# Thirty-two dense ranges instead of twenty-eight in a graph network's layer 1, with VectorE clearing the stored ranges and weighting late one-hots

## The reference

```python
x = ln(x + segment_sum(w_e * x[dst], src) @ W0.T)           # layer 0: sums by src
# layer 1: two graph convolutions, 128 and 64 features wide
deg  = in-degree + 1;  norm = deg[src]**-.5 * deg[dst]**-.5
h1 = relu(batch_norm(segment_sum(norm * (x @ W1)[src], dst) + b1))
h2 = relu(batch_norm(segment_sum(norm * (h1 @ W2)[src], dst) + b2))
x = ln(x + relu(concat(x, h1, h2) @ Wfc + bfc))
x = ln(x + mlp((1 + eps) * x + segment_sum(w_e * x[src], dst)))      # layer 2
x = ln(x + relu(ln(segment_sum(norm * (x @ W3)[src], dst) + b)))     # layer 3
```

## Time and profile before

| | us |
|---|---|
| median of 3 runs (3447.18 to 3460.74) | 3450.46 |
| the profiled execution | 3453.26 |
| its span, first to last instruction | 3452.0 |
| spread stage, first scatter to last | 45 to 1250 |
| layer 1's first pass (its POOL and PE work) | 1410 to 1749 |
| layer 1's second pass | 1794 to 2121 |
| layer 2's pass and tail | 2230 to 2935 |
| layer 3's pass and tail | 2935 to 3452 |
| busy: PE, POOL, DVE, ACT | 2833.8, 2463.3, 2001.4, 1170.1 |

### The profile page before, as it was taken

The page is one execution under the profiler, slowest core; times in us unless marked ns, Lnnn a source line. Parts: engine busy times, 40 slices in busy tenths (PEclk is TensorE's granted clock), DMA queues, the critical chain, the costliest instruction groups (busy, mean ns, idle before and its releaser), DMA issues. The chain is left out here.

```text
span 3452.0 us, 60131 instructions
## 1 busy us (share of the span) xinstructions
PE 2833.8 (82%) x19220; PEld 2088.0 (60%) x19220; DVE 2001.4 (58%) x7356; ACT 1170.1 (34%) x2749; POOL 2463.3 (71%) x2237
## 2 busy tenths in 40 slices
PE   5999877788888869789977997777888876699995
PEld 4777655566666648444446774356666665466664
DVE  7999888886777639442243434443444564235557
ACT  4354554566877748200010002500111232001113
POOL 3888778876776667677747776777777774777774
PEclk9999999999999979899978997589999998799997
DMA  8787888888888889678856886755556564988884
GB/s 273 112 142 107 150 158 153 158 154 174 181 174 174 178 185 347 180 211 234 236 132 177 227 223 171 217 174 156 163 177 182 161 177 122 299 237 247 251 250 141
DMA packets 658434, 652.77 MB, mean 189 GB/s; under 512 B 87902, under 2 KB 606476, under 8 KB 656588
## 3 DMA queue, kind: packets, MB, share of 16 engines
q0 software_dynamic: 153600, 258.41, 37.6%
q1 hardware_dynamic: 430670, 331.83, 31.2%
q10 hardware_dynamic: 73854, 58.70, 5.4%
HBM read 434.19 MB, written 214.52 MB: 188 GB/s over the span
## 5 line engine op out<-in xcount | busy, mean ns | idle before, releaser
L1680 POOL DMA_INDIRECT A<-rows_buf,big x572 | 900.6, 1574 | 327.8 <-issue 149.0
L880 POOL DMA_INDIRECT rows_buf<-T,idx x888 | 852.0, 959 | 275.9 <-issue 273.8
L974 PE MATMUL PSA<-S,rows_buf 128*128 128x128 bf16 (+2 forms) x5904 | 576.6, 252 | 217.9 <-DMA rows_buf<-X,idx 103.3
L974 PEld LDWEIGHTS PSA<-S,rows_buf 128*128 128x128 bf16 (+2 forms) x5904 | 515.9, 140 | 301.6 <-DMA rows_buf<-X,idx 82.4
L880 POOL DMA_INDIRECT rows_buf<-X,idx x528 | 508.2, 963 | 160.9 <-issue 159.4
L1030 DVE TENSOR_TENSOR accT<-PSA,accT 128x256 f32 (+2 forms) x354 | 132.6, 375 | 830.2 <-PE PSA L974 822.9
L1538 DVE TENSOR_TENSOR accT<-PSA,accT 128x392 f32 (+5 forms) x366 | 239.6, 655 | 168.1 <-PE PSA L1473 76.0
L1376 PE MATMUL PSA<-XRS,rows_buf 128*128 128x256 f32 x1144 | 311.2, 396 | 6.2 <-ACT rows_buf L1388 6.2
L791 ACT ACTIVATE accT<-accT,vec 128x500 f32<-128x500 f32 (+3 forms) x26 | 17.7, 694 | 668.4 <-DVE accT L789 668.3
L1388 ACT ACTIVATE rows_buf<-PSA 128x512 f32<-128x512 f32 x286 | 168.7, 594 | 203.9 <-PE PSA L1376 198.5
L1376 PEld LDWEIGHTS PSA<-XRS,rows_buf 128*128 128x128 f32 x1144 | 208.4, 196 | 31.3 <-ACT rows_buf L1367 6.6
(11 more groups left out here) (311 smaller groups left out, 5645.5 us busy)
## 6 DMA issues: line engine op xcount, KB each, us to landing
XRS<-Ad SPq DMA_DIRECT2D x400, 256.0 KB
Ad<-accT SPq DMA_DIRECT2D x224, 196.0 KB
XRS<-in_xpad SPq DMA_DIRECT2D x192, 128.0 KB
Awd<-accT SPq DMA_DIRECT2D x48, 392.0 KB
A<-accT SPq DMA_DIRECT2D x9, 1600.0 KB
rows_buf<-T,idx POOLq DMA_INDIRECT x888
rows_buf<-A SPq DMA_DIRECT2D x24, 512.0 KB
accT<-A SPq DMA_DIRECT2D x24, 512.0 KB, 6.4
```

Source lines behind the costliest of these rows:

```text
L880: s_hg[slot(i)][j // 2].on(pool.indirect_dma_start(Gv(slot(i), j), None, table, bass.IndirectOffsetOnAxis(idx[:, c:c + 1], 0)), 16)
L974: last = pe.matmul(PS[bank_of(i)][0:F, W * h:W * h + W], Gv(slot(i), j)[:, o:o + F], hits[:, i % SRING, j, :], start=j + part == 0, stop=j ...
L1680: s_k[n].on(pool.indirect_dma_start(A, bass.IndirectOffsetOnAxis(tgt[:, c:c + 1], 0), G[:, i % RING, j, :], None, compute_op=ALU.add), 16)
```

## The change

NWIN goes from 28 to 32. HOT becomes 556 chunks, the four new ranges are 32 units of one chunk with slots of 18, and layer 1's passes have 56 groups instead of 64 and eight quadruples of ranges instead of seven. The planner places the units anew: the hot ranges and the eleven beside them end at step 85 instead of 90, DENSE0 is 87 instead of 92, the last unit stays at step 137.

ACT no longer clears the ranges from HWIN on, nor `Aww`. DVE clears `Aww` in one int32 instruction per hot range and the 23 other range buffers that are used again in one bfloat16 instruction each, at the end of step s+4. The hot ranges' counts are still cleared on ACT with their flags; for the others the flag comes from the degrees: four small instructions in `add_flags` test whether a node from block 4 on has a degree over 250. In steps from DENSE0 on, DVE multiplies the one-hots by the weights, in one instruction of 128x512, and ACT does not.

```diff
@@ -40,7 +40,7 @@
 SPAN = 116
 MAXN = 20
 UC = NT * MAXN
-NWIN = 28
+NWIN = 32
 HWIN = 6
 OHRING = 6
 LEAD = 6
@@ -64,7 +64,7 @@
 HOT = BND[NWIN]
 FAR = 16384
 CLASSES = ((0, 64, 4, 8), (64, 120, 2, 8), (120, 160, 2, 10), (160, HOTW, 1, 8),
-           (HOTW, 376, 2, MAXN), (376, 448, 1, 14), (448, HOT, 1, 16))
+           (HOTW, 376, 2, MAXN), (376, 448, 1, 14), (448, 524, 1, 16), (524, HOT, 1, 18))
 G0 = BND[XWIN] // CG
 NCOLD = NG - 1 - G0
 ORDER = [x for i in range(HWIN) for x in (i, HWIN + i)][:2 * HWIN - 1]
@@ -179,6 +179,11 @@
 DENSE0 = cleared_at(HWIN - 1, 3) + 1
 
 
+CLEARED = [w for w in ORDER if w >= HWIN and any(user_before(q) == w for q in range(NWIN))]
+FARBLOCK = window_range(HWIN)[0] // 128
+MOSTDEGREE = 250
+
+
 def dense_step(t):
     return DENSE0 + t * (NCOLD - 2 - DENSE0) // NT
 
@@ -1312,6 +1317,11 @@
             if i >= 2:
                 v.wait_ge(s_M, i - 1)
             v.tensor_tensor(Su[:, i % 2, :, :], iota4, cur16[:, g:g + 1, :].broadcast_to([128, W, CG]), ALU.is_equal).then_inc(s_su, 1)
+            if i >= DENSE0:
+                v.wait_ge(s_su, i + 1)
+                c = CG * g
+                v.tensor_tensor(S[:, i % 2, :, :], Su[:, i % 2, :, :].rearrange("p w j -> p j w"),
+                                wgt[:, c:c + CG].unsqueeze(2).broadcast_to([128, CG, W]), ALU.mult).then_inc(s_sv, 1)
             v.wait_ge(s_sr, i + 1)
             for j in range(CG):
                 last = v.tensor_scalar(Eq[:, i % 2, j, :], PS[0][:, 128 * j:128 * j + 128], srcf[:, g, j:j + 1], 0.0,
@@ -1328,6 +1338,8 @@
 
         def weigh(i):
 
+            if i >= DENSE0:
+                return
             sc.wait_ge(s_su, i + 1)
             if i >= 2:
                 sc.wait_ge(s_M, i - 1)
@@ -1352,7 +1364,10 @@
             for j in range(CG):
                 last = pe.matmul(PS[1][:, 0:W], onesb[:, :], Su[:, i % 2, :, j], start=j == 0, stop=j == CG - 1)
             last.then_inc(s_hp, 1)
-            pe.wait_ge(s_sw, i + 1)
+            if i < DENSE0:
+                pe.wait_ge(s_sw, i + 1)
+            else:
+                pe.wait_ge(s_sv, i - DENSE0 + 1)
             pe.wait_ge(s_eq, i + 1)
             if i >= 1:
                 pe.wait_ge(s_mc, i)
@@ -1523,7 +1538,11 @@
             else:
                 v.wait_ge(s_ae, u.turns[half])
             if u.at - FIRST[u.w].at < 2 and user_before(u.w) is not None:
-                v.wait_ge(s_az, TURN[user_before(u.w)] + 1)
+                before = user_before(u.w)
+                if before < HWIN:
+                    v.wait_ge(s_az, before + 1)
+                else:
+                    v.wait_ge(s_azc, CLEARED.index(before) + 1)
             if u.at - FIRST[u.w].at < 2 and TURN[u.w] == LASTHOT + 2:
                 v.wait_ge(s_azw, HWIN)
             if half:
@@ -1549,17 +1568,23 @@
 
         def window_clear(w, i):
 
-            if w < HWIN and i in (0, 2):
-                sc.wait_ge(s_aww, 16 * (PARTS * w + (2 + i) * PARTS // 4))
-                for b in (i, i + 1):
-                    done = sc.activation(Aww[:, 1568 * b:1568 * b + 1568], nought[:, 0:1].broadcast_to([128, 1568]), ACT.Identity)
-                if i == 2:
-                    done.then_inc(s_azw, 1)
             sc.wait_ge(s_aw[TURN[w] % 2], 16 * (PARTS * (TURN[w] // 2) + (i + 1) * PARTS // 4))
             part = Aw[buffer_of(w)][:, 1568 * i:1568 * i + 1568]
             done = sc.activation(part, part, ACT.Relu, bias=neg255[:, 0:1], accum_out=full[:, 4 * w + i:4 * w + i + 1])
             if i == 3:
                 done.then_inc(s_az, 1)
+
+        def clear_weights(w):
+
+            v.wait_ge(s_aww, 16 * PARTS * (w + 1))
+            part = Aww.bitcast(I32)
+            v.tensor_scalar(part, part, 0, None, ALU.bitwise_and).then_inc(s_azw, 1)
+
+        def clear_counts(w):
+
+            v.wait_ge(s_aw[TURN[w] % 2], 16 * PARTS * (TURN[w] // 2 + 1))
+            part = Aw[buffer_of(w)]
+            v.tensor_scalar(part, part, 0.0, None, ALU.mult).then_inc(s_azc, 1)
 
         def dense_turn(t):
 
@@ -1650,17 +1675,13 @@
                     dense_turned(t)
                     if t + 2 < NT:
                         dense_load(sc, t + 2)
-            for w in ORDER:
+            for w in range(HWIN):
                 for k in range(4):
                     if i == cleared_at(w, k):
                         window_clear(w, k)
             if i == 10:
                 load_weights()
             transfers(i + 2)
-        for w in ORDER:
-            for k in range(4):
-                if cleared_at(w, k) > NCOLD:
-                    window_clear(w, k)
         for p in range(NCOLD + 3, NCOLD + 8):
             transfers(p)
 
@@ -1743,6 +1764,12 @@
                 for u in following[k:k + 1]:
                     onehots(u)
                 additions(us[k + 1:k + 2])
+            for w in range(HWIN):
+                if i == cleared_at(w, 2):
+                    clear_weights(w)
+            for w in CLEARED:
+                if i == cleared_at(w, 2):
+                    clear_counts(w)
             if i == 0:
                 unit_places_known()
             if i == 1:
@@ -1795,7 +1822,7 @@
         for i in range(2):
             sp.wait_ge(s_aw[i], 16 * PARTS * (NWIN // 2))
         v.wait_ge(s_da, NCOLD)
-        v.wait_ge(s_az, NWIN)
+        v.wait_ge(s_az, HWIN)
         v.wait_ge(s_azw, HWIN)
         settle_without_pool()
         for k in range(COPIES):
@@ -1994,6 +2022,11 @@
 
     def add_flags():
 
+        many = full[:, 4 * HWIN:4 * HWIN + 2]
+        link(v.memset(many, 1.0))
+        link(v.tensor_reduce(many[:, 0:1], dnm[:, FARBLOCK:NT - 1], AX.X, ALU.min))
+        link(v.tensor_copy(many[0:rows(NT - 1), 1:2], dnm[0:rows(NT - 1), NT - 1:NT]))
+        link(v.tensor_scalar(many, many, 1.0 / math.sqrt(MOSTDEGREE), None, ALU.is_lt))
         link(v.tensor_reduce(okf[:, 0:1], full[:, :], AX.X, ALU.add))
 
     def overflowed():
```

More of the change, by code:

```diff
@@ L273, in build @@
     early = big[:, 0:2 * LAST]
-    key = early[:, 5568:5568 + HOT]
-    srcm = early[:, 6112:6112 + HOT // 2].bitcast(BF16)
+    key = early[:, 5504:5504 + HOT]
+    srcm = early[:, 6096:6096 + HOT // 2].bitcast(BF16)
     iotak = early[:, 6384:6384 + UC // 2].bitcast(F16)
@@ L301, in build @@
     iota16 = sb("iota16", [128, W], BF16)
-    full = sb("full", [128, 4 * NWIN])
+    full = sb("full", [128, 4 * HWIN + 2])
     okf = sb("okf", [128, 2])
@@ L315, in build @@
     Su = early[:, 4800:5312].bitcast(BF16).rearrange("p (r w j) -> p r w j", r=2, j=CG)
-    lower = early[:, 5376:5504]
-    identb = early[:, 5504:5568].bitcast(BF16)
+    lower = early[:, 5312:5440]
+    identb = early[:, 5440:5504].bitcast(BF16)
     srcl = part[4].bitcast(BF16)[:, 784:1568]
@@ L1909, in build @@
     s_spread = count("s_spread")
-    s_ah, s_am, s_ae, s_az = (nc.alloc_semaphore(n) for n in ("s_ah", "s_am", "s_ae", "s_az"))
+    s_ah, s_am, s_ae, s_az, s_azc = (nc.alloc_semaphore(n) for n in ("s_ah", "s_am", "s_ae", "s_az", "s_azc"))
     s_su, s_sw, s_oq, s_amw, s_aew, s_azw, s_aww = (nc.alloc_semaphore(n) for n in ("s_su", "s_sw", "s_oq", "s_amw", "s_aew", "s_azw", "s_aww"))
     s_aw = [nc.alloc_semaphore(f"s_aw{i}") for i in range(2)]
+    s_sv = nc.alloc_semaphore("s_sv")
     ABW = [XS[:, 2 + i, :].bitcast(BF16) for i in range(2)]
```

## The result

The changed kernel takes 3503.99 us, median of 4 runs (3499.66 to 3509.54), where the kernel before takes 3452.57 on the same chip: a ratio of 1.0153 with a 95% interval of 1.0137 to 1.0169. It is 51 us slower, where 33 us faster was forecast, and lies outside the range. The profiled execution has a span of 3508.3 us. Every figure of a stage here comes from one profiled execution of each kernel.

| stage of the profiled execution, us | before | after | forecast | measured |
|---|---|---|---|---|
| start to degree addition of step 87 | 735.3 | 774.6 | +10 | +39.3 |
| step 87 to step 137 | 454.2 | 471.1 | -15 | +16.9 |
| step 137 to the last one, 142 | 33.5 | 28.7 | -5 | -4.8 |
| from there to the first gather of pass 1 | 187.3 | 193.7 | 0 | +6.4 |
| first pass, to the first gather of the second | 383.7 | 388.3 | +2 | +4.6 |

A forecast was written before the change was run, and what follows sets the result against it. POOL was taken to pace the early spread and layer 1's passes, waits over ACT's copies the late spread. 3453.3 us with 2 - 25 + 10 - 15 - 5 = -33 us gave 3420 us, range 3380 to 3465 us.

The forecast's parts named there:

- The late part: Spread stage, steps 87 to 137: 8.6 us per step, 439 us instead of 454, -15 us, bounds -46 and +25.
- term (d): Spread stage, DVE: 32 more units at 1.4 us each, 45 us; 0.4 us per late step.
- The early part: Spread stage, first 87 steps: 39 us added to DVE, which idles 94 of 705 us; +10 us, bounds 0 and +39.
- The tail: The six spread steps behind step 137, with no clears in ACT's way: -5 us, bounds 0 and -10.
- The first pass: Layer 1: eight groups fewer, but PE takes over at 5.86 us per step; 341 us against 339, +2 us.
- The second pass: Layer 1: DMA transfers at a 0.96 share set 5.3 us per step; 302 us against 327, -25 us.
- Rival 1: Spread stage: DVE's clears take POOL's time too, late steps stay at 9.4 us; +41 us, 3494 us, 12%.
- Rival 2: Layer 1 passes: DMA share no higher than 0.85, passes +16 and +8, spread -10; 3467 us, 13%.
- Rival 3: Spread stage: only ACT held late steps, now 8.1 us each, early clears fit idle time; -69 us, 3384 us, 14%.
- 4: Whole kernel: gains and costs cancel, spread +5 to +20, second pass -15 to -20; 3440 to 3458 us, 10%.
- 5: Layer 1 passes: new ranges' chunks spill over their slots, left-over loop runs 196 more rounds each; over 900 us more, 1%.
- my signs of being wrong: Late steps under 8.1 or over 9.2 us, scatters beside a clear over 3 us, or the second pass not shrinking.

The follow-up runs named there:

- the narrow units: Changed kernel with 32 ranges, first 12 turns spaced as with 28, instructions of the last four ranges' units 98 columns wide: 3501.95 us, 1.0127.
- 28 ranges respaced: Kernel before, nothing added, first 12 turns spaced as with 32 ranges, so the 12th ends with step 85: 3483.18 us, 1.0079.
- fewer bytes: Changed kernel loading half of each piece of counts in both layer 1 passes (but for the first pieces), all products done: 3470.90 us, 1.0068.
- less for TensorE: Changed kernel without the middle of three parts of each range's product in pass one and two of three products beside in pass two: 3444.21 us, 0.9987.
- the kernel with reductions: Changed kernel with DVE's clears, all but the sixth of Aww, replaced by one-port maximum reductions of nearly the same length: 3506.65 us, 1.0141.

## Why the prediction was wrong

- **The late part, the step that failed and cost most.** It was to fall to 8.6 us a step: 8.1 us of DVE's work and 0.5 us that I left DVE to idle. It took 9.4 (471.1 / 50). The work was right: DVE is busy 407.4 us of these, 8.15 a step. What failed is the idle time: 63.7 us, 1.27 a step. I had put the new units, term (d), into time in which DVE idles. The late parts of the kernel with the moves and 28 ranges and, in the second fence, with 32 ranges in the same spacing (columns as in the earlier trace rows) show that this didn't happen:

```profile
754.60:1216.60 462.00, 383.85 (x2555) 316.79 (x2554) 377.58 (x1224) 204.02 (x419) 354.60 (x212) 0.94 0.89 180
```

```profile
755.30:1267.70 512.40, 407.50 (x2619) 323.75 (x2618) 427.52 (x1332) 220.74 (x448) 358.83 (x212) 0.94 0.84 174
```

  Here DVE gets 49.9 us more to do, the part grows by 50.4, and the idle time stays, 84.4 and 84.9 us. The price of a unit was near (1.4 us of DVE's time, and it costs 1.6 us of the path), but it didn't vanish into idle time. Yet it isn't DVE's busy time as such: the narrow units take 23 us of it away (427.5 to 404.6), and the part takes 514.2 us. The part about ACT was right: with 28 ranges the same moves give 0.9949.
- **The early part: the number of steps.** I priced what DVE gets, 39 us, put it into the 94 us that DVE idles, and took +10. That DVE's load fits there was right where nothing else changes: with 28 ranges and the moves DVE is busy 659.2 us up to step 87 instead of 633.8, and step 87 comes at 734.5 us instead of 735.3. +39.3 is just my upper bound, but by luck: +44 stands in the kernel with ranges alone, where nothing is moved (step 87 at 779.5 us), and +46 in the one with 28 ranges respaced (780.8), where nothing is added either. I held the number of steps fixed and asked what they would cost. The part is paced by its units' turns, as the earlier trace rows could not show, and the plan took five steps out of it. The wait that shows this, TensorE's product for DVE's addition, was 72.7 us up to 755 us before; I read the waits of 750 to 1190 us alone. But with 32 ranges most of this +39.3 only says where the loss is seen: with the old spacing step 87 comes at 734.9 us, and the last step still only 6.7 us sooner.
- **The tail** was right (-4.8 against -5). The 6.4 us behind the last degree addition were not foreseen. This stretch is 191 to 196 us in all kernels with 32 ranges in the new spacing and 183 to 189 in all others, and why is open.
- **The first pass** came out near, +4.6 against +2, and TensorE takes over at 5.85 us, where 5.86 was worked out. In part this is luck: I had called the transfers nearly free here, and with fewer bytes the pass is 14 us shorter, so TensorE's work alone costs less than my sum and its waits for pieces fill the rest. POOL's timeline, the first gather of three groups in a row:

```profile
1715.20 0.94 POOL L885 DMA_INDIRECT rows_buf<-T,idx  x1 [1.20 <-PE PSA L979]
...
1721.05 0.95 POOL L885 DMA_INDIRECT rows_buf<-T,idx  x1 [1.16 <-PE PSA L979]
...
1726.90 0.94 POOL L885 DMA_INDIRECT rows_buf<-T,idx  x1 [1.15 <-PE PSA L979]
```

- **The second pass**: I took the larger of three limits (5.0, 5.15, 5.3), 5.3 us, and a free end. Each limit is about right, even the 0.96 of the DMA engines (0.95 seen with less for TensorE, 0.90 in the changed kernel); with either of two relieved TensorE ends at 5.2 to 5.3 us a group. Together they gave 5.8 us a group to TensorE's last product: (2176.0 - 1856.5 - 35) / 49. With limits so close the waits of one are not made up by another.
- **Rivals.** Rival 1 had the sign and nearly the size, +41, and its 9.4 us a late step, for the turn-taking and the clears. Its main cause was wrong: without clears 14 to 20 us come back, and the port costs nothing. Rival 2's ceiling of 0.85 is refuted by 0.95. Rival 3 is refuted for 32 ranges, as is 4, whose spread was to cost 5 to 20 us, and 5: its 900 us are not there. Of my signs of being wrong two came: late steps over 9.2 us, and a scatter beside a clear of 4.54 us, over 3. DVE from 750 to 1190 us is 87% busy, not over 90%.

## What to carry to other kernels

If a plan spreads units over the steps of a loop, adding units moves the old ones too: first ask which of the two paces each part, by counting steps and units in a window of the trace. Where units and steps take turns on in-order engines, don't put the work of more units into an engine's idle time: if that idle time is the waiting within each turn, it stays, and the work comes on top. And where three engines stand within 6% of each other in a loop, don't forecast the largest of their three limits; their waits can add to it.

## What the runs showed of the hardware

A `tensor_scalar` of DVE over 6272 elements a partition stretches a scatter of POOL by most of its own length. POOL's and then DVE's timeline after, at 250 us:

```profile
249.81 4.54 POOL L1701 DMA_INDIRECT A<-rows_buf,big  x1 [0.30 <-issue]
...
250.86 3.41 DVE L1581 TENSOR_SCALAR accT<-accT 128x6272 int32<-128x6272 int32 x1
```

1.54 us became 4.54 beside an instruction of 3.41 us, and the scatter ends at 254.35 us, 0.08 us behind it. In the forecast I had argued from a stretch of 0.48 us that this would be far less. By the Trainium skill, "SBUF — State Buffer", section "SBUF: two separate sides", the lock is held for a two-port instruction's whole length; the trace agrees. All in all it adds 44 us to the scatters' busy time, 900.6 to 945.0, and costs nothing here: the kernel with reductions is no faster, and POOL's idle time there is 44 us longer. POOL waited for others at least as long.
